# Softmax attentions with the maximum as ScalarE's bias and four output strips; a state-space step with its D term on TensorE

## Chip, cores, metric

One Trainium2 core runs the kernel. The metric is device time in microseconds (us) of the whole program; lower is better.

## What is computed

X holds 32 batches of 128 tokens with 128 numbers each. Six stages follow one another, and each ends with a layer norm over the last axis; cut to what the change touches:

```python
x = _layernorm(x + _L0_attn_ref(x, wq, wk, wv, wo))   # 1: 16 heads of 8, RoPE, causal
x = _layernorm(x + _L0_xattn_ref(ctx_1024, x, ...))   # 2: linear attention block
x = _layernorm(x + _L0_ffn_ref(x, ...))               # 3: routed experts
x = _layernorm(x + _L1_attn_ref(x, ...))              # 4: state space, below
x = _layernorm(x + _L1_xattn_ref(x, ctx_1024, ...))   # 5: 16 heads, 77 context keys
x = _layernorm(x + _L1_ffn_ref(x, ...))               # 6: experts chosen by sinkhorn

# 1 and 5, per batch and head
attn = softmax(Q @ K.T * scale + mask);  out = (attn @ V) @ wo.T

# 4: h is 256 x 16 numbers a batch, a recurrence over the 128 tokens
h = h * dA + dt_t * B_t * u_t;  y = einsum('bdn,bn->bd', h, C_t)
y = y_all + xc * D_param;  y = y * silu(z)
return x + y @ W_out                  # the caller adds x once more: 2 x + y @ W_out
```

All values are float32.

## The kernel before

X stays in SBUF. Every stage works on NG = 8 groups of GB = 4 batches, and each of the engines has a program of its own; semaphores link them. The first group of a stage is written out in a prelude, the others come from a loop body that also starts the next group.

**The attentions** (stage 1, names a_, and stage 5, names k_, one function `attention`) go through a group in 8 units u: half of the 16 heads of one batch. The order on each engine is written out by hand. TensorE forms the scores of 8 heads in two PSUM banks (L512; L515 adds the causal mask in stage 1), two units ahead. VectorE (`less_max`) takes the maximum of each head (L378, or L372 and L374 with the context's mask), then subtracts it and writes DD (L380, L376). ScalarE turns DD into E by one Exp over all 8 heads (L278). TensorE transposes E (L522), ScalarE copies the result to PT (L311), and TensorE multiplies by V (`outputs`, L533, 8 matmuls a unit into two strips of 32 columns of its array). VectorE sums E (L384). ScalarE does copy u, then Exp u + 1; the transposition of u + 1 waits for that Exp. One projection of the next group shares a unit's slot on TensorE (L490, L499 in stage 1, in units 1 to 5), its rotation by RoPE follows on VectorE (L391), and POOL builds the block-diagonal keys BD and the masked queries QM. In stage 5 ScalarE writes QM (L300). At a group's end come the reciprocal of the sums, the scaling of the outputs (rT on ScalarE, oT on VectorE L440), the matmuls by wo (L586), Y, statistics (L72), POOL's power and the norm (L90).

In the trace most float32 matmuls show up as two records (L533 as x16 for 8), transpositions as one.

**The state space** (stage 4, names m_, `state_space`) runs 32 steps per group, two channels (CH) by 16 states, through `pipeline`. Everything else of a group is hung on the steps by the table SLOT, which gives each part of the work a step number. A step: TensorE spreads B and C over the partitions (L1532, L1539), VectorE multiplies in PSUM by DU (L1447) and scans (L1452), ScalarE makes dA (L1405), POOL multiplies h by C (L1317), TensorE adds that up in a PSUM bank per channel (L1559, by the identity). After the last step of a group VectorE adds the D term (`gated`, L1457), multiplies by silu(z) (`gate`, L1462), TensorE projects (`output`), VectorE adds 2 X (`residual`, L1466), takes statistics (L72), POOL raises to the power, and VectorE normalises (`norm`, L90). These stand among the first steps of the next group.

**Openings.** In stage 1 a first block issues all of its loads on SP's queue and sets constants, then the prelude starts; POOL sets V to zero (L241) ahead of copying X. The four projections go through one bank, so each waits for the rotation before it. In stage 4 POOL folds the norm's weight into the convolution (L1290) ahead of the first inner norm, and `early` for group 1 runs ahead of step 0.

## Time and profile before

| what | value |
| --- | --- |
| median of 3 runs | 2200.84 us (2200.73 to 2204.45) |
| profiled execution | 2199.49 us, span 2197.7 us |
| mean granted TensorE clock | 0.867 |
| busy: TensorE, VectorE, ScalarE, POOL | 1684.6, 1584.7, 957.9, 826.3 us |
| stage 1, 2, 3 | 0 to 341, 341 to 600, 600 to 782 us |
| stage 4, 5, 6 | 782 to 1497, 1497 to 1784, 1784 to 2197.7 us |

The busy times are sums over stages that have different limits, so the table gives the frame only. A stage's limit is read from its own window: the busy time of each engine against the window's length, then who waits for whom inside one unit or one step. PEclk is the mean clock that TensorE was granted, 1.00 for 2.4 GHz and 0.50 for 1.2 GHz.

### The profile page before, as it was taken

What the parts mean: (1) busy time and instruction counts of PE and PEld (TensorE: products, weight loads), DVE (VectorE), ACT (ScalarE), POOL (GpSimd) and SP (SyncE); (2) the same over time, 40 slices, a digit from 0 to 9 for tenths busy, and PEclk for the clock granted to TensorE, in tenths of its full rate; (3) what the DMA queues carried; (4) which work ended last, traced back from release to release, by engine and by line L of the source; (5) the groups of instructions that cost most, each with busy time, mean ns of one, the idle gap of its engine ahead of it and who ended that gap; (6) DMA issues with size and microseconds to landing.
All of it is one profiled execution on the core that took longest, in us unless ns stands there. A gap on an engine that the chain in (4) does not pass through costs nothing. (4 is left out here: it accounts for less than half of the span.)

```text
span 2197.7 us, 31301 instructions
## 1 busy us (share of the span) xinstructions
PE 1684.6 (77%) x10064; PEld 1101.4 (50%) x10064; DVE 1584.7 (72%) x3014; ACT 957.9 (44%) x1509; POOL 826.3 (38%) x855
## 2 busy tenths in 40 slices
PE   6999986888699947777778778766999871289992
PEld 3555556877466622223223223214666661188882
DVE  3999995566478827988888888894989947833335
ACT  1444452454545435564564664643555432011114
POOL 2222211333300025665665665663222100066653
PEclk9999997788799968788888888897999975599996
DMA  4000000000000000000000000000000040076664
GB/s 127 1 0 0 0 1 24 1 1 2 1 1 0 0 10 0 1 0 2 0 0 1 0 0 0 0 0 10 7 3 6 1 130 0 9 232 204 198 203 122
DMA packets 48580, 71.47 MB, mean 33 GB/s; under 512 B 8877, under 2 KB 34581, under 8 KB 48197
## 3 DMA queue, kind: packets, MB, share of 16 engines
q1 hardware_dynamic: 43909, 60.64, 8.7%
q0 software_dynamic: 4544, 9.32, 1.5%
q8 instruction: 58, 0.95, 0.2%
q14 instruction: 69, 0.57, 0.1%
HBM read 58.46 MB, written 11.47 MB: 32 GB/s over the span
## 5 line engine op out<-in xcount | busy, mean ns | idle before, releaser
L1559 PE MATMUL PS<-m_hC,identf 128*128 128x512 f32 x512 | 330.0, 731 | 147.4 <-POOL m_hC L1317 142.2
L1317 POOL TENSOR_TENSOR m_hC<-m_h,m_Cs 128x512 f32<-128x512 f32 x256 | 337.1, 1325 | 223.9 <-DVE m_h L1452 154.3
L1452 DVE TENSOR_TENSOR_SCAN m_h<-m_dA,PS 128x512 f32<-128x512 f32 x256 | 312.4, 1220 | 29.6 <-ACT m_dA L1405 18.7
L1559 PEld LDWEIGHTS PS<-m_hC,identf 128*128 128x128 f32 x512 | 102.1, 223 | 289.9 <-POOL m_hC L1317 264.2
L1447 DVE TENSOR_TENSOR PS<-PS,m_DU 128x512 f32<-128x512 f32 x256 | 178.3, 697 | 29.5 <-PE PS L1532 16.3
L1405 ACT ACTIVATE m_dA<-m_DT,m_A 128x508 f32<-128x508 f32 x256 | 177.9, 716 | 28.5 <-DVE m_h L1452 22.5
L1410 ACT COPY m_Cs<-PS 128x512 f32<-128x512 f32 x128 | 74.2, 580 | 264.9 <-PE PS L1539 264.9
L1992 PE MATMUL PS<-e_xT,e_WT 128*128 128x128 f32 x1136 | 145.1, 282 | 13.0 <-DVE e_xT L1892 11.9
L1992 PEld LDWEIGHTS PS<-e_xT,e_WT 128*128 128x128 f32 x1136 | 136.4, 196 | 18.6 <-DVE e_xT L1892 17.3
L1765 ACT ACTIVATE e_Sg<-PS 128x512 f32<-128x512 f32 x71 | 42.3, 597 | 225.6 <-PE PS L1992 158.7
L1701 POOL DMA_INDIRECT e_XG<-token_rows,e_ids x71 | 68.8, 969 | 159.3 <-DVE e_ids L1886 138.0
L82 POOL TENSOR_TENSOR ln_lv<-ln_mv,ln_eps 128x4 f32<-128x4 f32 x32 | 6.4, 200 | 319.3 <-DVE ln_mv L75 319.3
L311 ACT COPY a_PT<-PS 128x1024 f32<-128x1024 f32 x63 | 63.8, 1012 | 88.1 <-PE PS L522 88.1
L1899 DVE TENSOR_TENSOR e_HT<-PS,e_Sg 128x512 f32<-128x512 f32 x71 | 49.1, 691 | 69.5 <-PE PS L1992 56.9
L1706 POOL DMA_INDIRECT expert_rows<-e_Yo,e_ids x71 | 69.9, 985 | 74.6 <-DVE e_Yo L1905 64.1
L278 ACT ACTIVATE a_E<-a_DD 128x1024 f32<-128x1024 f32 x64 | 67.7, 1057 | 55.0 <-DVE a_DD L380 53.8
L311 ACT COPY k_PT<-PS 77x1024 f32<-77x1024 f32 x63 | 63.4, 1007 | 61.8 <-PE PS L522 61.8
L522 PE MATMUL PS<-identf,k_E 128*77 128x128 f32 x512 | 71.4, 283 | 15.0 <-ACT k_E L278 14.9
L378 DVE TENSOR_REDUCE a_mx<-PS 128x8 f32<-128x1024 f32 x64 | 77.3, 1207 | 7.7 <-PE PS L515 7.7
L384 DVE TENSOR_REDUCE a_sm<-a_E 128x8 f32<-128x1024 f32 x64 | 77.4, 1210 | 5.4 <-ACT a_E L278 5.4
L1209 PEld LDWEIGHTS PS<-w_ew,f_G 128*128 128x128 f32 x512 | 64.7, 191 | 32.2 <-issue 26.0
L380 DVE TENSOR_TENSOR a_DD<-PS,a_mx 128x1024 f32<-128x1024 f32 x64 | 78.4, 1224 | 2.2
(374 smaller groups left out, 3926.4 us busy)
## 6 DMA issues: line engine op xcount, KB each, us to landing
e_WT<-in_w_wgu SPq DMA_DIRECT2D x71, 512.0 KB
token_rows<-X SPq DMA_DIRECT2D x2, 2048.0 KB
e_Y<-expert_rows SPq DMA_DIRECT2D x16, 256.0 KB, 3.9
e_w_wd<-in_w_wd SPq DMA_DIRECT2D x1, 2048.0 KB, 8.3
out_dram<-X SPq DMA_DIRECT2D x8, 256.0 KB, 2.3
X<-in_x SPq DMA_DIRECT2D x1, 1792.0 KB, 7.6
x_Cs<-in_ctx SPq DMA_DIRECT2D x8, 154.0 KB
k_Cs<-in_ctx SPq DMA_DIRECT2D x8, 154.0 KB
```

What stands on the lines that cost most here:

```text
L311: nc.scalar.copy(PT[:, u % 2], PS[0:KL, 4:6, :].rearrange("p i (h q) -> p (i h) q", q=P)).then_inc(s["pt"], 1)
L378: nc.vector.tensor_reduce(m, units(hf), AX_X, ALU.max).then_inc(s["mx"], 1)
L380: nc.vector.tensor_tensor(d, units(hf), mb, ALU.subtract).then_inc(s["d"], 1)
L384: nc.vector.tensor_reduce(sm[:, u * HU:(u + 1) * HU], E[:, u % 2], AX_X, ALU.add).then_inc(s["sm"], 1)
L522: ins = nc.tensor.transpose(PS[0:KL, 4 + h // 4, (h % 4) * P:(h % 4 + 1) * P], E[:, u % 2, h, :], c.identf[:, :])
L1317: nc.gpsimd.tensor_tensor(hC[:, i % ND, :], hst[:, i % ND, :], Cs[:, n % ND, :], ALU.mult).then_inc(s["hC"], 1)
L1405: nc.scalar.activation(dA[:, i % ND, :, 1:P], bl(DT[:, par, ch, :])[:, :, 1:P], ACT.Exp, scale=A[:, ch, n:n + 1]).then_inc(s["dA"], 1)
L1410: nc.scalar.copy(Cs[:, n % ND, :], bank(3)).then_inc(s["Cs"], 1)
L1447: nc.vector.tensor_tensor(bank(4), bank(1 + n % 2), DU[:, par, ch, :], ALU.mult).then_inc(s["dBu"], 1)
L1452: nc.vector.tensor_tensor_scan(hst[:, i % ND, :], dA[:, i % ND].rearrange("p b l -> p (b l)"), bank(4), 0.0, ALU.mult, ALU.add).then_inc(s ...
L1559: nc.tensor.matmul(bank(5 + ch), c.identf[:, :], hC[:, i % ND, :], start=(n == 0), stop=(n == NS - 1)).then_inc(s["yacc"], 1)
L1992: ins = nc.tensor.matmul(PS[:, banks[i % 2], f * P:(f + 1) * P], WT[:, i % RW, w, f * P:(f + 1) * P], xT[:, i % 2, :], start=True, stop=True)
```

## The change

Softmax. For the upper 4 of a unit's 8 heads VectorE only takes the maximum and multiplies it by -SCALE (a new 128x4 operation, nmx); ScalarE takes this as the bias of four Exps, one for each head, that read the scores themselves (PSUM in stage 1, DD with the mask in stage 5). For the lower 4 heads subtraction and Exp stay, at half size. `outputs` runs once per batch, after its second unit, as 16 matmuls over four strips in turn; PT has four buffers. The maxima of both first units of the next group stand ahead of oT on VectorE.

Stage 4. The D term is a matmul by a diagonal matrix Dp that opens each channel's accumulation, and 2 X comes from a matmul by `twice` that opens the projection's. VectorE keeps the product by silu(z), from PSUM, and statistics from PSUM. ScalarE does the norm of the group, with POOL making its bias by two small products more. The channels of the convolution's projection change places.

Openings. V is set to zero by VectorE; the first projections have banks of their own and don't wait for a rotation; in stage 1 loads are split over SP's and ScalarE's queues, and the separate first block is gone; in stage 4 the fold comes after the first inner norm, and `early` for group 1 after step 0 (VectorE), 1 (POOL), 3 (TensorE) or 4 (ScalarE). ScalarE loads its Exp table early. `keep_warm` issues 9 to 14 bf16 matmuls of 128x512 into an unused bank at the start of stages 1 and 4 and at the end of stages 1, 2, 4 and 5.

```diff
+def keep_warm(c, n, at):
+    for i in range(n):
+        nc = c.nc
+        nc.tensor.matmul(c.PS[:, at, :], c.warm[:, 0:P], c.warm[:, :], start=True, stop=True)
...
-    for stages, g in ((early, 0), (prepare, 0), (early, 1)):
+    for stages in (early, prepare):
         for stage in stages.values():
-            stage(g, g)
-    for i in range(shift):
-        step(0, 0, i, 2)
+            stage(0, 0)
+    for i in range(-1, shift):
+        if i >= 0:
+            step(0, 0, i, 2)
+        if i == second:
+            for stage in early.values():
+                stage(1, 1)
...
-    PT = sb("PT", [KL, 2, HU, P])
+    PT = sb("PT", [KL, 4, HU, P])
...
-                nc.gpsimd.memset(V[:, :, :, :], 0.0).then_inc(s["z"], 1)
...
             def exps(g, u):
+                act.wait_ge(s["nm"], g * UN + u + 1)
+                for j in range(HG):
+                    src = DD[:, u % 2, HG + j, :] if cross else PS[:, 2 * (u % 2) + 1, j * KL:(j + 1) * KL]
+                    nc.scalar.activation(E[:, u % 2, HG + j, :], src, ACT.Exp, bias=nmx[:, u % 2, j:j + 1], scale=SCALE)
                 act.wait_ge(s["d"], g * UN + u + 1)
-                nc.scalar.activation(E[:, u % 2], DD[:, u % 2], ACT.Exp, scale=SCALE).then_inc(s["e"], 1)
+                nc.scalar.activation(E[:, u % 2, 0:HG], DD[:, u % 2, 0:HG], ACT.Exp, scale=SCALE).then_inc(s["e"], 1)
...
+                act.wait_ge(s["o_ready"], g * GB + u // 2)
+                nc.scalar.copy(PT[:, u % 4], PS[0:KL, 4:6, :].rearrange("p i (h q) -> p (i h) q", q=P)).then_inc(s["pt"], 1)
...
-                    dve.wait_ge(s["mx"], at)
-                    nc.vector.tensor_tensor(d, d, mb, ALU.subtract).then_inc(s["d"], 1)
                 else:
                     nc.vector.tensor_reduce(m, units(hf), AX_X, ALU.max).then_inc(s["mx"], 1)
-                    dve.wait_ge(s["mx"], at)
-                    nc.vector.tensor_tensor(d, units(hf), mb, ALU.subtract).then_inc(s["d"], 1)
+                dve.wait_ge(s["mx"], at)
+                nc.vector.tensor_scalar(nmx[:, hf, :], mx[:, hf, HG:HU], -SCALE, 0.0, ALU.mult, ALU.add).then_inc(s["nm"], 1)
+                nc.vector.tensor_tensor(DD[:, hf, 0:HG], DD[:, hf, 0:HG] if cross else scores(2 * hf), mb, ALU.subtract).then_inc(s["d"], 1)
...
+                nc.vector.memset(V[:, :, :, :], 0.0).then_inc(s["zv"], 1)
+                dve.wait_ge(s["zv"], 1)
                 dve.wait_ge(wsem, wcount)
-                dve.wait_ge(s["z"], 2)
+                if cross:
+                    values(0, 0, FIRST_V + 1)
+                else:
+                    for i in range(4):
+                        rotate(0, i, i)
+                    dve.wait_ge(s["rot"], 4)
+                    nc.vector.tensor_tensor(QM[:, 0, :], R[:, 2, :], R[:, 3, :], ALU.add).then_inc(s["q"], 1)
                 if xsem is not None:
                     dve.wait_ge(xsem[0], 16)
...
                         if left:
                             less_max(g + 1, 1 - par, 0)
+                            less_max(g + 1, 1 - par, 1)
                     if left:
                         if cross:
...
                 if left:
-                    less_max(g + 1, 1 - par, 1)
...
-            def outputs(g, par, u):
-                hf, b = u % 2, u // 2
-                pe.wait_ge(s["pt"], g * UN + u + 1)
-                if u == 0:
+            def outputs(g, par, b):
+                pe.wait_ge(s["pt"], g * UN + 2 * b + 2)
+                if b == 0:
                     pe.wait_ge(s["v"], g + 1)
-                for h in [i % 2 * HG + i // 2 for i in range(HU)]:
-                    gp, j = 2 * hf + h // HG, h % HG
-                    ins = nc.tensor.matmul(PS[32 * gp:32 * gp + 32, OUT, b * P:(b + 1) * P], V[:, par, b * 4 + gp, 32 * j:32 * j + 32], PT[:, u % 2, h, :],
-                                           start=(j == 0), stop=(j == HG - 1))
+                for j in range(HG):
+                    for gp in range(4):
+                        ins = nc.tensor.matmul(PS[32 * gp:32 * gp + 32, OUT, b * P:(b + 1) * P], V[:, par, b * 4 + gp, 32 * j:32 * j + 32],
...
+                else:
+                    pe.wait_ge(s["xT"], 1)
+                    for i, w in enumerate(("wk", "wkp", "wq", "wqp")):
+                        nc.tensor.matmul(bank(i), W[w][:, :], xT[:, :], start=True, stop=True).then_inc(s["kp"], 1)
+                    project_values(0, FIRST_V)
...
                         ins.then_inc(s["rTp"], 1)
-                    outputs(g, par, u)
+                    if u % 2 == 0:
+                        outputs(g, par, u // 2 - 1)
                 if left:
                     pe.wait_ge(s["pt"], g * UN + UN)
                     transpose_p(g + 1, 0)
+                outputs(g, par, GB - 1)
+                if left:
...
+            keep_warm(c, 14, 0)
...
-    SLOT = {"gated": 1, "silu_z": 1, "gate": 2, "output0": 2, "output1": 3, "rstd": 5, "residual": 6, "norm": 7,
+    SLOT = {"silu_z": 1, "gate": 1, "output0": 2, "output1": 3, "rstd": 5, "stats": 5, "norm": 9,
...
+                if isinstance(g, int) and g == 0:
+                    fold()
...
+                for ch in range(CH):
+                    nc.scalar.activation(Dp[:, ch, :], c.identf[:, :], ACT.Copy, scale=W["dp"][:, ch:ch + 1]).then_inc(s["tw"], 1)
+                nc.scalar.activation(twice[:, :], c.identf[:, :], ACT.Copy, scale=2.0).then_inc(s["tw"], 1)
...
+            def norm(g, par):
+                act.wait_ge(s["nb"], g + 1)
+                for b in range(GB):
+                    ins = nc.scalar.activation(X[:, bass.ds(g * GB + b, 1), :].rearrange("p o d -> p (o d)"), PS[:, 7, b * D:(b + 1) * D], ACT.Identity, scale=ln["rs"][:, b:b + 1], bias=no[:, 1, b:b + 1])
+                ins.then_inc(s["x"], 1)
...
-            def gated(g, par):
+            def gate(g, par):
                 dve.wait_ge(s["yacc"], g * NI + NI)
+                dve.wait_ge(s["sz"], g + 1)
                 for ch in range(CH):
-                    nc.vector.scalar_tensor_tensor(YG[:, ch, :], U2[:, par, ch, :], W["dp"][:, ch:ch + 1], bank(5 + ch), ALU.mult, ALU.add).then_inc(s["y1"], 1)
-            def gate(g, par):
-                dve.wait_ge(s["y1"], g * 2 + 2)
-                dve.wait_ge(s["sz"], g + 1)
-                nc.vector.tensor_tensor(YG[:, :, :], YG[:, :, :], SZ[:, par], ALU.mult).then_inc(s["y2"], 1)
-            def residual(g, par):
+                    nc.vector.tensor_tensor(YG[:, ch, :], bank(5 + ch), SZ[:, par, ch, :], ALU.mult).then_inc(s["y1"], 1)
+            def out_stats(g, par):
                 dve.wait_ge(s["yp"], g + 1)
-                nc.vector.scalar_tensor_tensor(flat(Xn[:, :, :]), flat(group(c, g)), 2.0, bank(7), ALU.mult, ALU.add).then_inc(s["r2"], 1)
-                dve.wait_ge(s["r2"], g + 1)
-                ln_stats(dve, nc, Xn, ln, s, g + 1)
-            def norm(g, par):
-                ln_apply(dve, nc, group(c, g), Xn, ln, s, g + 1, s["x"])
+                ln_stats(dve, nc, bl(bank(7)), ln, s, g + 1)
...
                         pe.wait_ge(s["xnT"], g + 1)
-                        if not isinstance(g, int) or g > 0:
-                            pe.wait_ge(s["zc"], g * CH)
+                    if ch == 0 and half == 0 and (not isinstance(g, int) or g > 0):
+                        pe.wait_ge(s["zc"], g * CH)
+                        pe.wait_ge(s["x"], g)
...
-                if n == 0 and not (isinstance(g, int) and g == 0):
-                    pe.wait_ge(s["y1"], g * 2 - 1 + ch)
+                if n == 0:
+                    if not (isinstance(g, int) and g == 0):
+                        pe.wait_ge(s["y1"], g * 2 - 1 + ch)
+                    nc.tensor.matmul(bank(5 + ch), Dp[:, ch, :], U2[:, par, ch, :], start=True, stop=False)
                 pe.wait_ge(s["hC"], g * NI + i + 1)
-                nc.tensor.matmul(bank(5 + ch), c.identf[:, :], hC[:, i % ND, :], start=(n == 0), stop=(n == NS - 1)).then_inc(s["yacc"], 1)
+                nc.tensor.matmul(bank(5 + ch), c.identf[:, :], hC[:, i % ND, :], start=False, stop=(n == NS - 1)).then_inc(s["yacc"], 1)
...
+                    pe.wait_ge(s["y1"], g * 2 + 2)
                     for b in (2 * half, 2 * half + 1):
+                        nc.tensor.matmul(PS[:, 7, b * D:(b + 1) * D], twice[:, :], X[:, bass.ds(g * GB + b, 1), :].rearrange("p o d -> p (o d)"), start=True, stop=False)
                         for ch in range(CH):
-                            ins = nc.tensor.matmul(PS[:, 7, b * D:(b + 1) * D], YG[:, ch, b * P:(b + 1) * P], W["wout"][:, ch, :], start=(ch == 0), stop=(ch == CH - 1))
+                            ins = nc.tensor.matmul(PS[:, 7, b * D:(b + 1) * D], YG[:, ch, b * P:(b + 1) * P], W["wout"][:, ch, :], start=False, stop=(ch == CH - 1))
...
+            keep_warm(c, 12, 1)
...
-        def later_loads(sp):
+        def first_load(eng, *names):
+            for n in names:
+                eng.dma_start(Ws[1][n][:, :], dram[f"w1_{n}"]).then_inc(sem[1], 16)
+        def first_sp(sp):
+            sp.dma_start(c.X[:, 0:GB, :], dram["x"][:, 0:GB, :]).then_inc(s_x, 16)
+            first_load(sp, "wk", "wq", "cos", "hmask", "wv", "wo")
...
+        def first_act(act):
+            nc.scalar.dma_start(c.identf[:, :], dram["identf"]).then_inc(s_identity, 16)
+            first_load(nc.scalar, "wkp", "wqp", "sin", "cmask")
...
+        def first_pe(pe):
+            pe.wait_ge(s_warm, 1)
+            keep_warm(c, 9, 6)
+            pe.wait_ge(s_identity, 16)
```

Order of instructions on TensorE within a group of stage 1, units 2 and 3, before (a_E are the exponentials, a_PT their transposed copy, PS is PSUM):

```order
L533 MATMUL PS<-a_PT,a_V 32x128 x8
L520 REGISTER_ALU
L522 MATMUL PS<-identf,a_E 128x128 x8
L512 MATMUL PS<-a_BD,a_QM 128x512 x2
L515 MATMUL PS<-w_cmask,identb 128x512 x2
L489 REGISTER_ALU
L490 MATMUL PS<-a_xT,w_wq 128x512
L533 MATMUL PS<-a_PT,a_V 32x128 x8
L520 REGISTER_ALU
L522 MATMUL PS<-identf,a_E 128x128 x8
L512 MATMUL PS<-a_BD,a_QM 128x512 x2
```

and in the changed kernel:

```order
L557 MATMUL PS<-a_PT,a_V 32x128 x16
L545 REGISTER_ALU
L547 MATMUL PS<-identf,a_E 128x128 x8
L537 MATMUL PS<-a_BD,a_QM 128x512 x2
L540 MATMUL PS<-w_cmask,identb 128x512 x2
L513 REGISTER_ALU
L514 MATMUL PS<-a_xT,w_wq 128x512
L545 REGISTER_ALU
L547 MATMUL PS<-identf,a_E 128x128 x8
L537 MATMUL PS<-a_BD,a_QM 128x512 x2
L540 MATMUL PS<-w_cmask,identb 128x512 x2
L513 REGISTER_ALU
```

One call of the output matmuls now has 16 of them, and the unit that follows has none.

ScalarE in the same stage, two units, before:

```order
L311 COPY a_PT<-PS 128x1024
L277 REGISTER_ALU
L278 ACTIVATE a_E<-a_DD 128x1024
L311 COPY a_PT<-PS 128x1024
L277 REGISTER_ALU
L278 ACTIVATE a_E<-a_DD 128x1024
```

and in the changed kernel:

```order
L327 COPY a_PT<-PS 128x1024
L329 REGISTER_ALU
L289 REGISTER_ALU
L292 ACTIVATE a_E<-PS,a_nmx 128x128 x4
L294 ACTIVATE a_E<-a_DD 128x512
L326 REGISTER_ALU
L327 COPY a_PT<-PS 128x1024
L289 REGISTER_ALU
L292 ACTIVATE a_E<-PS,a_nmx 128x128 x4
L294 ACTIVATE a_E<-a_DD 128x512
```

Between two copies there stood one Exp, and now there are five in two forms, the four small ones behind VectorE's a_nmx.

VectorE behind the last step of a group in stage 4, before:

```order
L1451 REGISTER_ALU
L1452 SCALAR_TENSOR_TENSOR m_h<-m_dA,PS 128x512
L1457 SCALAR_TENSOR_TENSOR m_YG<-m_U,w_dp,PS 128x512 x2
L1444 REGISTER_ALU
L1447 TENSOR_TENSOR PS<-PS,m_DU 128x512
L1448 REGISTER_ALU
L1451 REGISTER_ALU
L1452 SCALAR_TENSOR_TENSOR m_h<-m_dA,PS 128x512
L1462 TENSOR_TENSOR m_YG<-m_YG,m_SZ 128x1024
```

and some steps later, the residual, the statistics and the first of four norms:

```order
L1466 ISA
L1466 SCALAR_TENSOR_TENSOR m_Xn<-X,PS 128x512
L72 BN_STATS ln_st<-m_Xn 128x6 x4
L75 BN_AGGR ln_mv<-ln_st 128x2 x4
L1447 TENSOR_TENSOR PS<-PS,m_DU 128x512
L1448 REGISTER_ALU
L1452 SCALAR_TENSOR_TENSOR m_h<-m_dA,PS 128x512
L90 TENSOR_SCALAR X<-m_Xn,ln_mv,ln_rs 128x128
L90 ISA
```

In the changed kernel the same two places on VectorE read:

```order
L1512 REGISTER_ALU
L1513 SCALAR_TENSOR_TENSOR m_h<-m_dA,PS 128x512
L1519 TENSOR_TENSOR m_YG<-PS,m_SZ 128x512 x2
L1505 REGISTER_ALU
L1508 TENSOR_TENSOR PS<-PS,m_DU 128x512
L1509 REGISTER_ALU
L1512 REGISTER_ALU
L1513 SCALAR_TENSOR_TENSOR m_h<-m_dA,PS 128x512
```

and, for the second, the statistics straight from PSUM:

```order
L1508 TENSOR_TENSOR PS<-PS,m_DU 128x512
L1509 REGISTER_ALU
L1513 SCALAR_TENSOR_TENSOR m_h<-m_dA,PS 128x512
L72 BN_STATS ln_st<-PS 128x6 x4
L75 BN_AGGR ln_mv<-ln_st 128x2 x4
L1505 REGISTER_ALU
L1508 TENSOR_TENSOR PS<-PS,m_DU 128x512
L1509 REGISTER_ALU
```

The product by m_SZ moved up from the second step to the first and absorbed the D term's place; m_Xn, the residual and the norm's L90 are gone from this engine.

## Rows read from the trace of the kernel before

**Rows 1.** Busy time by engine; window, length, busy and count each, clock, DMA.

```profile
79.60:335.10 255.50, 236.99 (x1842) 142.02 (x1842) 232.76 (x294) 121.91 (x129) 58.08 (x62) 0.99 0.00 0
793.30:803.50 10.20, 10.13 (x16) 4.04 (x16) 0.00 (x0) 1.97 (x2) 0.00 (x0) 0.70 0.00 0
926.00:1490.80 564.80, 422.21 (x952) 163.82 (x950) 488.12 (x603) 299.90 (x464) 344.76 (x270) 0.84 0.00 0
1554.30:1778.70 224.40, 200.52 (x1736) 151.78 (x1736) 201.37 (x348) 119.74 (x159) 53.87 (x63) 0.99 0.01 4
```

**Rows 2.** Timeline, stage 1: start, length, engine, work, [idle before].

```profile
135.54 1.07 PE L533 MATMUL PS<-a_PT,a_V 128*32 128x128 f32 x16
...
136.54 1.09 PE L522 MATMUL PS<-identf,a_E 128*128 128x128 f32 x8
...
141.05 1.09 PE L522 MATMUL PS<-identf,a_E 128*128 128x128 f32 x8
...
142.18 1.01 ACT L311 COPY a_PT<-PS 128x1024 f32<-128x1024 f32 x1 [2.30 <-PE PS L522]
...
143.08 1.06 ACT L278 ACTIVATE a_E<-a_DD 128x1024 f32<-128x1024 f32 x1
```

**Rows 3.** ScalarE by form: busy us, mean ns, idle before, releasers.

```profile
L278 ACT ACTIVATE a_E<-a_DD 128x1024 f32<-128x1024 f32 x64 | 67.7, 1057 | 55.0 <-DVE a_DD L380 53.8
...
L278 ACT ACTIVATE k_E<-k_DD 128x616 f32<-128x616 f32 x64 | 45.9, 718 | 48.2 <-DVE k_DD L376 47.3
...
L1773 ACT ACTIVATE e_Y<-e_Y,e_E 128x128 f32<-128x128 f32 x32 | 10.1, 387 | 10.8 <-DMA e_Y<-expert_rows 10.8
```

**Rows 4.** VectorE by form, the same columns.

```profile
L380 DVE TENSOR_TENSOR a_DD<-PS,a_mx 128x1024 f32<-128x1024 f32 x64 | 78.4, 1224 | 2.2
...
L376 DVE TENSOR_TENSOR k_DD<-k_DD,k_mx 128x616 f32<-128x616 f32 x64 | 55.4, 866 | 2.2
...
L90 DVE TENSOR_SCALAR X<-m_Xn,ln_mv,ln_rs 128x128 f32 x24 | 16.0, 726 | 0.0
...
L90 DVE TENSOR_SCALAR X<-a_Y,ln_mv,ln_rs 128x128 f32 x24 | 6.7, 342 | 0.0
```

**Rows 5.** Timeline, stage 5, two plain units and the queries.

```profile
1599.40 2.77 ACT L300 ACTIVATE k_QM<-PS,k_bqm,w_gmask 128x512 f32<-128x512 f32 x4
...
1604.25 1.10 PE L522 MATMUL PS<-identf,k_E 128*77 128x128 f32 x8
...
1607.44 1.10 PE L522 MATMUL PS<-identf,k_E 128*77 128x128 f32 x8
```

**Rows 6.** Timeline of VectorE, end of one group of stage 4.

```profile
1083.20 1.41 DVE L1457 SCALAR_TENSOR_TENSOR m_YG<-m_U,w_dp,PS 128x512 f32<-128x512 f32 x2 [1.01 <-PE PS L1559]
...
1086.47 1.20 DVE L1462 TENSOR_TENSOR m_YG<-m_YG,m_SZ 128x1024 f32<-128x1024 f32 x1
...
1095.55 0.66 DVE L1466 SCALAR_TENSOR_TENSOR m_Xn<-X,PS 128x512 f32<-128x512 f32 x1
...
1099.34 2.67 DVE L90 TENSOR_SCALAR X<-m_Xn,ln_mv,ln_rs 128x128 f32 x4
```

**Rows 7.** Costliest groups of the page, the one that sums in PSUM.

```profile
L1559 PE MATMUL PS<-m_hC,identf 128*128 128x512 f32 x512 | 330.0, 731 | 147.4 <-POOL m_hC L1317 142.2
```

**Rows 8.** Timeline, opening of stage 1.

```profile
7.29 4.36 POOL L241 MEMSET a_V<- 128x5120 f32 x1
...
29.00 2.08 PE L512 MATMUL PS<-a_BD,a_QM 32*128 32x512 f32 x4
```

**Rows 9.** Timeline, opening of stage 4.

```profile
785.36 2.34 POOL L1290 TENSOR_TENSOR m_Wc<-m_Wc,w_win 128x1024 f32<-128x1024 f32 x1 [3.52 <-DMA m_Wc<-in_w_cwr]
...
830.51 0.70 DVE L1447 TENSOR_TENSOR PS<-PS,m_DU 128x512 f32<-128x512 f32 x1 [6.37 <-PE PS L1532]
```

**Rows 10.** Timeline, opening of stage 5.

```profile
1496.77 4.36 POOL L241 MEMSET k_V<- 77x5120 f32 x1
...
1513.80 1.75 PE L512 MATMUL PS<-k_BD,k_QM 128*128 128x308 f32 x3
```

181 lines of the change are left out of this document (97 added, 84 removed).

## Prediction

> **What bounds the kernel now.** I read the windows first (busy time per engine in the steady part of three stages), then the timeline of single units inside them, then the rows of the operations that the change touches, and last the three openings. Everything is summed against the profiled execution, 2199.49 us (span 2197.7); the median of the runs is 2200.84, so 1.35 us is added at the end. A measurement of this kernel tells about 0.2% (4.4 us) from no change.
>
> In stage 1 [rows 1] seven groups take 255.50 us (36.5 each). TensorE is busy 236.99 of it and VectorE 232.76: two engines at over 90%, ScalarE under half. So neither limit alone can be removed with profit. Stage 5 is the same picture at 224.40 us (32.1 a group), 200.52 and 201.37. In stage 4 seven groups take 564.80 us (80.7 each); VectorE is busy 488.12, TensorE 422.21, POOL 344.76, ScalarE 299.90. VectorE leads, and its idle 76.7 us (11 a group) are waits on others. TensorE's accumulation there waits 147.4 us, 142.2 of them for POOL's product [rows 7], and POOL's product waits for VectorE's scan: time given back by VectorE goes down this line.
>
> In stage 1 the units come in two kinds. Where a projection shares the slot, TensorE runs without a gap, 4.51 us from one transposition to the next, of which the output matmuls take 1.00 [rows 2]. Where there is none, VectorE's three passes of about 1.22 [rows 4] make 3.66. Beside both runs a loop of ScalarE and TensorE: transposition at 141.05, copy 142.18, Exp 143.08, which needs 1.06, then the next transposition: 2.03 + 1.06 + 0.07 of release = 3.16, hidden so far. In stage 5 the plain units stand 3.19 apart [rows 5].
>
> **Attentions, ScalarE's part.** Two Exps of different sizes [rows 3] give the slope: (1057 - 718) / (1024 - 616) = 0.83 ns an element, 0.21 us fixed. The half left over costs 0.63 (512 elements) or 0.46 (308). A 128x128 piece with one pointer operand has a row, 387 ns, so 0.28 fixed; of 77 elements, 0.345. Neighbours overlap by about 0.1: four queries of 771 ns would be 3.08 and take 2.77 [rows 5], with [rows 3] giving the fixed part. So stage 1: 4x0.387 + 0.63 - 0.4 = 1.78, +0.72 over 1.06. Stage 5: 4x0.345 + 0.46 - 0.4 = 1.44, +0.72 over 0.72. Without overlap each is 0.4 more (bound above). The loop becomes 2.03 + 1.78 + 0.07 = 3.88 in stage 1 and 3.54 in stage 5.
>
> **VectorE's part.** The subtraction halves: 1.22 to about 0.66, 0.87 to about 0.46. Added is the 128x4 scaling of the maximum. It has no row: below it costs nothing, above the 0.34 us of L90's 32 times larger scaling. I take 0.1, nearer the first, plus a chance to wait for POOL. The rows for that are L90's too: the same operation on the same shape takes 342 ns behind the attention and 726 in stage 4 [rows 4]; POOL is busy 23% and 61% of those windows [rows 1]. At 23% I take 0.1 us more a unit. Net -0.35 a unit in stage 1, -0.2 in stage 5. A plain unit of stage 1 then costs VectorE 3.66 - 0.35 = 3.31, less than the loop's 3.88: it no longer bounds.
>
> The Trainium skill, page "SBUF — State Buffer", says that VectorE and GpSimd arbitrate for one port pair by an exclusive lock held for the full instruction. The two L90 rows agree. Read strictly it speaks against this change: each of 128 new scalings could stand behind one whole GpSimd instruction, and ScalarE waits for it.
>
> **TensorE's part.** Two units have 32 records of output matmuls, before in two calls over two strips each, now in one over four strips. Two strips give 16 records in 1.00 [rows 2]. Four are bounded by no better rate (2.0 for 32) and by twice the rate (1.0); I take 1.3 against 2.0, nearer the second. So two units with projections: before 9.02. After, the one without outputs is no longer PE's 3.51 but the loop's 3.88; the other is 3.51 + 1.3 = 4.81. Together 8.69, -0.33; two such pairs, -0.66. Plain units: 3.66 to 3.88, +0.22, three of them, +0.66. At the boundary both maxima of the next group now stand ahead of oT, so the VectorE wait for ScalarE's rT is filled: the order shows it, and I take -0.6. Per group -0.6, over seven **-4**.
>
> The Trainium skill, page "TensorEngine Tiling (Array Packing)", section Theoretical Speedup, gives 4x tiling for a small dimension of 32 and "Up to 4×". By it 32 matmuls would take the 1.0 of my lower bound, and the stage would gain 0.3 more per pair. No row here shows four strips, so the trace can't confirm it.
>
> Stage 5: plain units 3.19 to 3.54, three a group, +1.05. The queries (2.77 on ScalarE) lie between one Exp and the next copy; they were just covered, and an Exp that ends 0.72 later pushes the copy by that: +0.7. Output slots -0.35, boundary -0.2. +1.2 a group, **+9** over seven (rounded up for the last).
>
> **Stage 4.** Gone from VectorE per group [rows 6]: the D term 1.41, the gate 1.20, the residual 0.66, the last norm 2.67, 5.94 in all. New: two half gates, by the size of the old one 2x0.7 = 1.4. Net -4.5 busy. The statistics read PSUM in place of SBUF at the same price. The norm's slot is also one in which POOL and VectorE collided (726 against 342), so some more comes back from POOL; I take -5.2 a group, **-36** over seven. What arrives elsewhere: TensorE gets two 128x512 matmuls, four records at 0.64 (330.0 over 512, [rows 7]), and four small ones, about 3.5 us of the 20 us a group that it is idle; ScalarE gets four norms, some 0.4 each as the piece with one pointer, 1.6 of 38 idle. If either stands ahead of a step, it takes part back: ends -20 and -42.
>
> **Openings.** Stage 1: the memset of V holds POOL 4.36 us from 7.29, and the copy of X that starts everything stands behind it; the four projections then wait for each rotation; the first score comes at 29.00 [rows 8]. With the load order, four banks and the sum of the queries on VectorE I follow: X at about 4 (an estimate: half of what stands ahead of it now), transposed and copied by 6.5, four projections until 15 if each takes the 2.08 that the score takes at the low clock, rotation and sum to 16: -13. The first scores, 2.08 each now, may run at the full clock, and the first group has the new slots: -4. VectorE's memset of 5120 elements must end before its first rotation; at 1.2 ns an element it would take 6 us from 1, just hidden. **-17** (-12 to -22).
>
> Stage 4: the fold of the convolution (POOL waits 3.52 and works 2.34, [rows 9]) leaves the chain to the inner norm; its statistics are ready within the first part: -4.2. Sixteen projections run 10.13 us at a mean clock of 0.70 [rows 1]; at full clock 7.1: -3. VectorE's first step waits 6.37 for TensorE, which stands behind the second group's transposition; now that comes after some steps: -5 of 6.37. **-12** (-9 to -14).
>
> Stage 5: the same memset 4.36 ahead of X [rows 10]; the score at 1513.80. Memset -4.3; of the 12.7 us that then remain until the score, an earlier table load and separate banks take about a third, -4.5 (an estimate, no row has them apart); less 2 for the first group's longer Exps: **-7** (-5 to -10).
>
> Filler matmuls at the ends of stages 1, 2, 4 and 5: 9 to 14 short ones in a time in which TensorE had nothing. They can give only what the low clock cost later; by the 3 us of stage 4 I take **-4** in all for stages 2, 3 and 6, ends 0 and -10.
>
> **Sum.** -4 + 9 - 36 - 17 - 12 - 7 - 4 = -71. 2199.5 - 71 = 2128.5, plus 1.35 is about 2130; I say 2129.
>
> **Rivals.**
> 1. As summed, 2129: chance 0.52. Its own range is 2112 to 2146.
> 2. VectorE's relief in stage 4 is half eaten. For it: TensorE waits 142.2 us for POOL [rows 7], VectorE already idles 11 us a group. A POOL backlog, or the D matmul ahead of a step's sum, would take the VectorE time as a wait. Against it: POOL is only 61% busy. The stage gives -20 in place of -36: 2145. Chance 0.18.
> 3. The attentions go below the sum: four strips cost the lower bound, and VectorE's relief counts in full. 0.35 us a unit over 64 units is 22 less in stage 1, and the +9 vanishes: 2100. Against it is the loop of 3.88. Chance 0.11.
> 4. The attentions get slower by the loop: the pieces do not overlap, +0.4 in each unit that the loop bounds, about half of 128: +26, 2155. For it: nothing in the trace has Exps with a pointer on PSUM back to back. Against it: the queries' 2.77 for four. Chance 0.14.
> 5. Slower than before: the loop's place is ScalarE between copy and transposition, 128 times. To eat the -71 it must cost 0.55 us a unit more than summed (71/128), that is Exp parts of 2.3 us in stage 1 with every other term right. With each scaling stuck behind a whole POOL product, which holds ScalarE back by the same time, that could be 0.65 a unit: 2129 + 83 = 2212. The rows speak against it, as POOL is busy 23% there. Chance 0.04.
> 6. The change does little: stage 4 limited by POOL, openings by the loads. 2200. Chance 0.01.
>
> **Numbers.** The range takes in cases 1 to 4 but for their outer ends: 2095 to 2162. Faster by over 0.2%: 0.95; within: 0.01; slower: 0.04.
>
> **What would show it.** Right: the plain units of stages 1 and 5 stand 3.9 and 3.5 apart with ScalarE, not VectorE, released last; 32 output matmuls in 1.3; a stage 4 group at about 75.5; first score near 16. Wrong: scaling rows of over 0.3 us, output matmuls at 2 us for 32, stage 4 still over 78 a group with more idle time before VectorE's sum or TensorE's accumulation, or stage 1 at 34 a group, where I have put the loop too high. The biggest single term is stage 4's; an error there of half its size is more than all openings' bounds together.

## The result and the profile after

The changed kernel takes 2143.74 us (median of 4 runs, 2141.09 to 2149.92) against 2202.62 for the kernel before in the same comparison: ratio 0.9737, 95% interval 0.9712 to 0.9761. That is 58.9 us less, where 71 were forecast; it lies inside the range. The profiled execution was the longest of the four, 2149.92 us with a span of 2148.1, while that of the kernel before (2199.49) was shorter than any of the four beside it (2200.73 to 2204.45). So the two traces differ by 49.6 us, and the other 9.3 are in no stretch below.

The trace of both kernels was cut at the same instructions: the first and the last sum Y of an attention, the first inner statistics, the first step and the first and last gate of stage 4, the first Exp of stage 5, the first copy of an expert's rows.

| stretch | before | after | moved | forecast |
| --- | --- | --- | --- | --- |
| start to first Y of stage 1 | 79.6 | 59.9 | -19.7 | -17 |
| seven groups of stage 1 | 255.5 | 250.7 | -4.8 | -4 |
| from there to stage 4 | 446.9 | 445.8 | -1.1 | part of -4 |
| opening of stage 4 to the first step | 48.5 | 35.7 | -12.8 | -12 |
| first step to first gate | 82.4 | 84.8 | +2.4 | none |
| seven groups of stage 4 | 573.1 | 550.4 | -22.7 | -36 |
| last gate to first Y of stage 5 | 68.3 | 63.5 | -4.8 | -7 |
| seven groups of stage 5 | 224.4 | 239.0 | +14.6 | +9 |
| from there to stage 6's expert rows | 148.3 | 145.1 | -3.2 | part of -4 |
| stage 6's experts to the end | 270.7 | 273.2 | +2.5 | none |

The three steady stretches in the changed kernel's trace (window, length, busy time and count of TensorE, its weight loads, VectorE, ScalarE and POOL, then clock and DMA). Stages 1 and 5 before are in [rows 1]. The window of stage 4 in [rows 1] runs from the first to the last statistics of the output (564.80 us); cut at the gates as the table has it, the kernel before gives the first line here:

```profile
912.90:1486.00 573.10, 429.52 (x969) 166.78 (x968) 498.67 (x615) 305.14 (x472) 351.10 (x275) 0.85 0.00 1
```

```profile
59.90:310.60 250.70, 220.37 (x1858) 125.67 (x1860) 211.88 (x347) 152.19 (x344) 58.14 (x62) 0.96 0.00 1
876.90:1427.30 550.40, 432.87 (x1053) 168.47 (x1052) 469.29 (x574) 314.37 (x500) 349.08 (x289) 0.88 0.00 0
1490.80:1729.80 239.00, 179.25 (x1752) 132.85 (x1754) 192.01 (x400) 157.16 (x374) 51.18 (x63) 0.97 0.01 4
```

In stage 1 VectorE lost 20.9 us of work and TensorE 16.6, and the time only 4.8. In stage 5 TensorE lost 21.3 and VectorE 9.4, and the stage grew, while ScalarE went from 119.74 to 157.16. The operations behind it, ScalarE by form (busy us, mean ns, idle before):

```profile
L292 ACT ACTIVATE a_E<-PS,a_nmx 128x128 f32<-128x128 f32 x256 | 73.4, 374 | 20.8 <-DVE a_nmx L397 20.0
L292 ACT ACTIVATE k_E<-k_DD,k_nmx 128x77 f32<-128x77 f32 x256 | 71.0, 352 | 18.6 <-DVE k_nmx L397 17.9
...
L294 ACT ACTIVATE a_E<-a_DD 128x512 f32<-128x512 f32 x64 | 41.7, 651 | 0.0
...
L294 ACT ACTIVATE k_E<-k_DD 128x308 f32<-128x308 f32 x64 | 28.6, 448 | 0.0
```

and VectorE's new and halved ones:

```profile
L398 DVE TENSOR_TENSOR a_DD<-PS,a_mx 128x512 f32<-128x512 f32 x64 | 43.7, 682 | 0.0
L398 DVE TENSOR_TENSOR k_DD<-k_DD,k_mx 128x308 f32<-128x308 f32 x64 | 30.6, 478 | 0.0
...
L397 DVE TENSOR_SCALAR k_nmx<-k_mx 128x4 f32<-128x4 f32 x64 | 17.1, 268 | 2.2
...
L397 DVE TENSOR_SCALAR a_nmx<-a_mx 128x4 f32<-128x4 f32 x64 | 14.0, 219 | 2.2
```

The forecast had 387 and 345 ns for a piece of 128 and 77 elements, 0.63 and 0.46 us for the rest, and for the scaling 0.1 bare with 0.1 more for POOL. The pieces are right (374 and 352 ns, 0.65 and 0.45 us), the scaling takes 0.22 and 0.27 us. Two plain units of stage 5 (units without a projection), from the timeline:

```profile
1542.70 1.10 PE L547 MATMUL PS<-identf,k_E 128*77 128x128 f32 x8
...
1543.84 1.01 ACT L327 COPY k_PT<-PS 77x1024 f32<-77x1024 f32 x1 [1.19 <-PE PS L547]
1544.74 1.11 ACT L292 ACTIVATE k_E<-k_DD,k_nmx 128x77 f32<-128x77 f32 x4
...
1545.75 0.45 ACT L294 ACTIVATE k_E<-k_DD 128x308 f32<-128x308 f32 x1
...
1546.25 1.10 PE L547 MATMUL PS<-identf,k_E 128*77 128x128 f32 x8 [1.41 <-ACT k_E L294]
1546.54 0.17 DVE L397 TENSOR_SCALAR k_nmx<-k_mx 128x4 f32<-128x4 f32 x1
...
1548.32 1.08 PE L557 MATMUL PS<-k_PT,k_V 77*32 77x128 f32 x32
...
1549.88 1.10 PE L547 MATMUL PS<-identf,k_E 128*77 128x128 f32 x8 [0.48 <-ACT k_E L294]
```

From one transposition to the next it is 3.55 and 3.63 us: copy, four Exps on the bias, one Exp, transposition. ScalarE is released by TensorE and TensorE by ScalarE, while VectorE's scaling for the next unit (at 1546.54) is done 1.7 us before it is wanted. Before, two such units stood 3.19 apart [rows 5]. This holds for plain units: over each attention ScalarE's first Exp still waited 15 times for the scaling, 20.0 and 17.9 us in all (the rows of L292 above). The line with x32 answers to the x16 of [rows 2]: 32 records of output matmuls in 1.08 us where 16 took 1.07.

VectorE at the end of a stage 4 group, which answers to [rows 6]:

```profile
1040.97 1.29 DVE L1519 TENSOR_TENSOR m_YG<-PS,m_SZ 128x512 f32<-128x512 f32 x2 [0.93 <-PE PS L1616]
...
1050.68 0.89 DVE L72 BATCH_NORM_STATS2 ln_st<-PS 128x6 f32<-128x128 f32 x4 [0.44 <-PE PS L1624]
```

Four pieces of work with 5.94 us became one with 1.29. The first score of stage 1 stands at 15.91, against 29.00 in [rows 8]:

```profile
4.43 0.61 POOL L235 COPY a_Xs<-X 128x512 f32<-128x512 f32 x1 [3.60 <-DMA X<-in_x]
...
7.10 1.10 PE L574 MATMUL PS<-a_xT,w_wk 128*128 128x512 f32 x2 [0.77 <-ACT a_xT L298]
...
9.75 1.02 PE L574 MATMUL PS<-a_xT,w_wqp 128*128 128x512 f32 x2
...
15.91 1.36 PE L537 MATMUL PS<-a_BD,a_QM 32*128 32x512 f32 x4 [4.24 <-POOL a_BD L247]
```

X is copied at 4.43, the projections follow one another without a rotation in between and at the full clock, and what holds the score is POOL's BD, not the projections. In stage 4 the first step no longer waits for TensorE [rows 9] but for POOL's product:

```profile
792.13 0.70 DVE L1508 TENSOR_TENSOR PS<-PS,m_DU 128x512 f32<-128x512 f32 x1 [2.46 <-POOL m_DU L1354]
```

### The profile page after: what moved, and what is told of

Its sections match the earlier page's. It is cut to its first block and busy times, and to the rows that moved or that the text cites. A ratio compares the mean times of both kernels' runs of the same rounds, so it can differ in the third digit from the quotient of the medians.

```text
span 2148.1 us, 32305 instructions
## 1 busy us (share of the span) xinstructions
PE 1651.6 (77%) x10228; PEld 1063.9 (50%) x10233; DVE 1525.8 (71%) x3098; ACT 1049.6 (49%) x2056; POOL 813.2 (38%) x868
## 5 line engine op out<-in xcount | busy, mean ns | idle before, releaser
L1362 POOL TENSOR_TENSOR m_hC<-m_h,m_Cs 128x512 f32<-128x512 f32 x256 | 332.6, 1307 | 216.4 <-DVE m_h L1513 152.0
L1616 PE MATMUL PS<-m_hC,identf 128*128 128x512 f32 x512 | 319.9, 710 | 116.3 <-POOL m_hC L1362 115.7
L547 PEld LDWEIGHTS PS<-identf,k_E 128*77 128x77 f32 x512 | 56.5, 149 | 75.4 <-ACT k_E L294 53.9
L327 ACT COPY k_PT<-PS 77x1024 f32<-77x1024 f32 x63 | 63.5, 1008 | 56.9 <-PE PS L547 56.9
L547 PE MATMUL PS<-identf,a_E 128*128 128x128 f32 x512 | 72.7, 287 | 23.3 <-ACT a_E L294 21.7
L292 ACT ACTIVATE a_E<-PS,a_nmx 128x128 f32<-128x128 f32 x256 | 73.4, 374 | 20.8 <-DVE a_nmx L397 20.0
```

What stands on the lines that cost most here:

```text
L292: nc.scalar.activation(E[:, u % 2, HG + j, :], src, ACT.Exp, bias=nmx[:, u % 2, j:j + 1], scale=SCALE)
L327: nc.scalar.copy(PT[:, u % 4], PS[0:KL, 4:6, :].rearrange("p i (h q) -> p (i h) q", q=P)).then_inc(s["pt"], 1)
L547: ins = nc.tensor.transpose(PS[0:KL, 4 + h // 4, (h % 4) * P:(h % 4 + 1) * P], E[:, u % 2, h, :], c.identf[:, :])
L1362: nc.gpsimd.tensor_tensor(hC[:, i % ND, :], hst[:, i % ND, :], Cs[:, n % ND, :], ALU.mult).then_inc(s["hC"], 1)
L1616: nc.tensor.matmul(bank(5 + ch), c.identf[:, :], hC[:, i % ND, :], start=False, stop=(n == NS - 1)).then_inc(s["yacc"], 1)
```

## The experiments

The runs came in three sets of four, and the kernel before ran on the same chip as each set: 2173.41 us (median) beside the first, 2173.47 beside the second and 2199.75 beside the third. So ratios are compared between sets, and microseconds only inside a set or inside a stretch of a trace. A stretch is read from one execution each: the one from stage 1 to stage 4, which no experiment but the one without fillers edits, took 441.0 to 445.9 us in the twelve traces, so a difference of a few microseconds in one stretch needs more than one trace to stand. The sets are: the changed kernel again, the old end, the bias in stage 1 alone, the filler; then no bias, both gains, tail and order, no filler matmuls; then the rest.

**The changed kernel again.** No edit.

> The changed kernel once more, nothing edited, as the yardstick of its neighbours and for a second profile. Its first profiled execution took 2149.92 us and its median was 2143.74. Theory: the 6 us between them lie in stage 4, where the groups alternate between 79.3 us at a clock of 0.89 and 84.8 at 0.84, so an execution with other dips is shorter there by a multiple of about 5.5. Rival: they lie in stage 6, where the profile was 2.5 us longer than that of before. Median expected at 2144.

Median 2120.07 us where 2144 was expected, ratio 0.975 (0.9728 to 0.9773). Every stretch but one repeats within 3.5 us: stage 1 250.5, stage 4 549.2, stage 5 240.7. The last one, stage 6's experts, took 243.6 in place of 273.2; these 29.6 us are the whole difference between the two traces (spans 2148.1 and 2118.7), and no edit touches that stage. The 6 us between the first profile and its median are not placed by this, neither by the theory nor by its rival: stage 4 gave only 1.2.

**The old end of a stage 4 group.**

```diff
-    SLOT = {"silu_z": 1, "gate": 1, "output0": 2, "output1": 3, "rstd": 5, "stats": 5, "norm": 9,
+    SLOT = {"gated": 1, "silu_z": 1, "gate": 2, "output0": 2, "output1": 3, "rstd": 5, "residual": 6, "norm": 7,
...
-                    nc.tensor.matmul(bank(5 + ch), Dp[:, ch, :], U2[:, par, ch, :], start=True, stop=False)
...
-                        nc.tensor.matmul(PS[:, 7, b * D:(b + 1) * D], twice[:, :], X[:, bass.ds(g * GB + b, 1), :]...)
```

with `gated`, `gate`, `residual` and `norm` on VectorE as before, and the norm gone from ScalarE.

> The changed kernel with the end of a stage 4 group as it was: D term, gate, residual and norm on VectorE, no matmuls by Dp and twice. If the change of this part is worth what the two profiles say (573.1 against 550.4 us over seven groups), it is 20 to 25 us slower than the changed kernel, about 2167. If the gain of the whole came from the openings and the part was worth the -36 that was forecast, only hidden by something else, 2180. If VectorE's relief is worth nothing there, 2145. Its groups should take 82 to 85 us again with 71 to 72 us of VectorE busy in each.

Median 2148.96, 28.9 above its neighbour; ratio 0.9884 (0.9864 to 0.9904). The seven groups take 580.7 us against 549.2: by these two traces the part is worth **31.5 us**, by the medians 28.9, near the 36 of the forecast. The profiled execution (2156.62) was the longest of its four. And 580.7 is 7.6 above the 573.1 of the kernel before, which has the same tail. One group of it:

```profile
882.20:967.50 85.30, 65.60 (x145) 25.81 (x144) 72.47 (x91) 46.27 (x72) 52.00 (x42) 0.82 0.00 1
```

**Tail and order of the channels.** The same with the projections of channel 0 first:

```diff
-                      "x0": project_x(1, 0), "x1": project_x(1, 1), "x2": project_x(0, 0), "x3": project_x(0, 1)
+                      "x0": project_x(0, 0), "x1": project_x(0, 1), "x2": project_x(1, 0), "x3": project_x(1, 1)
```

> The old end of a stage 4 group on the changed kernel took 580.7 us over seven groups, 7.6 more than the kernel before, which has the same tail. Here the projections of the convolution go back to channel 0 first as well. If the order of channels costs the 7.6, the seven groups take 573; if it is the clock that falls otherwise, they stay between 578 and 583, and the clock of the groups says so.

Median 2149.13, ratio 0.9889 (0.9866 to 0.9911), seven groups 580.6: the order costs nothing. In the kernel before, two of the first five groups took 82.3 us at a clock of 0.85 and three 85.0 to 85.2 at 0.82, with the same 72.5 us of VectorE; with the old tail under the new opening all five take 85.1 to 85.5. The changed kernel has such pairs too:

```profile
956.20:1041.00 84.80, 67.21 (x157) 26.23 (x156) 68.41 (x86) 47.58 (x76) 51.72 (x44) 0.84 0.00 0
1041.00:1120.20 79.20, 62.23 (x157) 24.64 (x156) 68.28 (x86) 47.71 (x76) 51.74 (x44) 0.89 0.00 0
```

84.8 and 79.2 us for the same work on VectorE. So in the one trace of the kernel before two groups had a better clock. Both profiles with the old tail were the longest of their four executions, and that of the kernel before was a short one; how many such groups the other executions have isn't known. So the part is worth 29 to 32 us by its reversal and 22.7 by the two first profiles, and the 7.6 between them are a difference between single executions.

**A filler in stage 4.**

```diff
                 if not first(g, n, 1):
                     pe.wait_ge(s["Cs"], g * NS + n)
+                keep_warm(c, 1, 3)
```

> The changed kernel with one bf16 matmul of 128x512 more ahead of each spreading of C in stage 4, into the bank that it is about to overwrite: 16 a group, some 0.21 us each at the full clock. Theory, the clock: groups at 0.89 take 79.3 us and those at 0.84 take 84.8 with the same VectorE work, so if the fillers keep the clock up, up to 5 us in every second group is won, 5 to 25 us in all, and the mean clock of the stage rises from 0.88 towards 1.0. Rival, TensorE's time: 16 matmuls add 3.4 us a group to TensorE, 27 in all, and the time grows by 5 to 25.

Median 2110.83, 9.2 below its neighbour; ratio 0.9712 (0.9695 to 0.9728). Two groups:

```profile
876.10:955.10 79.00, 63.05 (x172) 25.81 (x172) 68.18 (x86) 46.97 (x76) 51.64 (x43) 0.94 0.00 1
955.10:1037.80 82.70, 67.14 (x172) 27.32 (x172) 68.12 (x86) 47.38 (x76) 51.66 (x43) 0.86 0.00 1
```

The seven groups take 544.9 us, 4.3 less, at a mean clock of 0.92 against 0.88. The other 5 us of the medians aren't in the edited stage. The theory holds in its sign; its size, 5 to 25 us, is just missed. TensorE's busy time is 430.6 us against 430.2, with 110 records more. And the mean clock of a group doesn't tell its time: the fourth group took 82.0 us at 0.94, and the first 79.0 at the same 0.94.

```profile
1116.10:1198.10 82.00, 63.02 (x173) 25.58 (x172) 68.25 (x87) 47.64 (x76) 51.67 (x43) 0.94 0.00 0
```

**The bias in stage 1 alone.** In stage 5:

```diff
+                if cross:
+                    act.wait_ge(s["d"], g * UN + u + 1)
+                    nc.scalar.activation(E[:, u % 2], DD[:, u % 2], ACT.Exp, scale=SCALE).then_inc(s["e"], 1)
+                    return
```

and the subtraction over all eight heads on VectorE.

> The changed kernel, but in stage 5 VectorE subtracts the maximum for all eight heads and ScalarE takes one Exp of 616 elements, as before the change; stage 1 keeps its bias. Theory: the loop of ScalarE and TensorE bounds stage 5 (3.55 and 3.63 us a unit in the profile against 3.19 before), so it is faster by 10 to 22 us: the four strips stay and the longer Exps go. A group then takes 31 to 32 us in place of 34.0. Rival, VectorE bounds it: its 0.27 us scaling goes and 0.4 comes back, so the time stays within 3 us or grows.

Median 2096.77, 23.3 below its neighbour; ratio 0.9642 (0.9622 to 0.9661). Stage 5's seven groups fall from 240.7 to 223.4 us, 17.3 less. Of this the last group alone gives 6.3 (35.2 to 28.9). One group with the bias (the changed kernel), then one without:

```profile
1524.80:1558.70 33.90, 26.24 (x256) 19.26 (x256) 28.13 (x59) 23.54 (x56) 8.11 (x10) 1.00 0.02 5
```

```profile
1517.70:1549.60 31.90, 26.10 (x256) 19.26 (x256) 29.61 (x51) 17.73 (x24) 8.61 (x10) 1.00 0.02 5
```

VectorE works 1.5 us more and ScalarE 5.8 less, and the group is 2.0 shorter. So it is ScalarE's part, not VectorE's sum. Everything else that the change did to stage 5 is worth 224.4 - 223.4 = 1.0, and more where the clock holds: two of the seven groups here were at 0.95, and in the run with both gains (below), where none was, they took 221.1.

**No bias at all.** The same for both attentions.

> The changed kernel with the whole subtraction on VectorE and one Exp for eight heads in both attentions; strips, order and openings stay. Stage 5 is known from its neighbour: 223.4 us for seven groups against 240.7. Open is stage 1. If the bias pays there, its seven groups go from 250.5 back to 255 or more. If, as in stage 5, the loop of ScalarE costs more than VectorE gets back, and the 4.8 us won in stage 1 came from the four strips, they go below 250.5, to about 242. As a ratio to the kernel before: 0.966 in the first case, 0.960 in the second.

Median 2106.35, ratio 0.9696 (0.9675 to 0.9718). Stage 1 takes 259.2 us against 250.5, so here the bias is worth 8.7. That sum has three parts: 1.4 us in each of the first six groups at the full clock (8.4), some 3 for two groups more at a lower clock in this run, and 2.7 the other way, as the last group took 33.4 without the bias and 36.1 with it. The first two groups behind the opening without it, and the same two with it:

```profile
62.20:100.40 38.20, 33.32 (x272) 19.18 (x272) 34.48 (x43) 17.99 (x19) 9.40 (x10) 0.96 0.01 2
100.40:137.00 36.60, 31.91 (x272) 17.88 (x272) 34.50 (x44) 17.99 (x19) 9.40 (x10) 1.00 0.00 0
```

```profile
62.20:97.40 35.20, 31.79 (x272) 17.90 (x272) 31.34 (x52) 22.50 (x51) 9.41 (x10) 1.00 0.00 1
97.40:134.30 36.90, 33.59 (x272) 19.13 (x272) 31.40 (x52) 22.41 (x51) 9.40 (x10) 0.95 0.00 0
```

At the full clock it is 36.6 against 35.2, and before the change 37.2. Each kind has groups with a dip, a short stretch at 1.2 GHz, that takes the mean clock to 0.95 or 0.96, in which 1.6 to 1.7 us more pass, with VectorE's work unchanged. The kernel before had a clock of 1.00 in its first six groups.

**The scaling twice.**

```diff
+                nc.vector.tensor_scalar(nmx2[:, hf, :], mx[:, hf, HG:HU], -SCALE, 0.0, ALU.mult, ALU.add)
                 nc.vector.tensor_scalar(nmx[:, hf, :], mx[:, hf, HG:HU], -SCALE, 0.0, ALU.mult, ALU.add).then_inc(s["nm"], 1)
```

> The changed kernel with VectorE's scaling of the maximum issued twice, the first time into a buffer that nobody reads: 0.17 to 0.27 us more of VectorE in each of 128 units, ahead of ScalarE's bias. If VectorE, or the wait of ScalarE for the scaling, bounds the units, stages 1 and 5 grow by 0.2 a unit, 13 us each. If the loop of ScalarE and TensorE bounds them, the scaling of the next unit is done long before the copy of this one, and each grows by less than 4. In stage 5 plain units the scaling ends 1 us ahead of the Exp that needs it, so I expect the second there; in stage 1 VectorE is nearer, some 5 us.

Median 2155.31, ratio 0.9805 (0.9788 to 0.9822). A steady group of stage 1 and one of stage 5:

```profile
62.20:97.60 35.40, 31.78 (x272) 17.88 (x272) 31.81 (x60) 22.54 (x51) 9.42 (x10) 1.00 0.01 1
1596.50:1631.30 34.80, 26.22 (x256) 19.26 (x256) 29.66 (x68) 23.54 (x56) 7.71 (x10) 1.00 0.02 5
```

35.4 against 35.2, and 34.8 against 33.9. The doubled scaling costs 0.2 us in a stage 1 group and 0.9 in one of stage 5, where 8 times 0.17 to 0.27 would be 1.4 to 2.1. So VectorE is not the bound of stage 1's units, where I had expected some 5 us in all and none came (250.3 against 250.5). In stage 5 about half of it comes through, more than the 4 us that I had set as the bound (seven groups 246.6 in place of 240.7). So VectorE isn't free there: the waits of ScalarE's first Exp for the scaling went from 15 times and 17.9 us in the changed kernel to 21 times and 21.8 us. The ratio grew by about 12 us; the profile places 6 to 8 of them.

**No filler matmuls.** `keep_warm` issues none.

> The changed kernel with none of the filler matmuls (starts of stages 1 and 4, ends of stages 1, 2, 4 and 5). Forecast: 4 us slower, between 0 and 10. Where each acts is read from the openings: 35.7 in stage 4 (3 of them by the clock), 145 from the last group of stage 5 to the first rows of stage 6, 60 to the first output of stage 1. The rival is that the clock rises at the same moment anyway, then it is within 1 us.

Median 2125.48, ratio 0.9791 (0.9765 to 0.9817). The ratio is 0.004 or 9 us above the changed kernel's, with intervals that overlap; the medians lie 5.4 apart, with the kernel before at the same median beside both, and the two traces 4.0. So the fillers' worth as a whole is on the edge of noise. By stretch: opening of stage 4 38.2 against 35.8, stage 5's 38.9 against 37.3, into stage 6 148.5 against 147.0, first Y 63.7 against 62.2. In the opening of stage 1 the cause is in the rows: the first projection (at 6.68) took 2.05 us, where it took 1.10 with the fillers. Against these 7 us, stage 1's groups took 247.5 in place of 250.5, with none of the first six at a lower clock. So where the dips of the clock fall is not fixed by the work of a group.

**The second group's early parts first.**

```diff
+    second = -1
     for i in range(-1, shift):
```

> The changed kernel with the early parts of the second group ahead of step 0 again on all engines, as before the change. Opening of stage 4 (first statistics to first step) 35.8 us now; forecast of this term was -5, so it should be 40.8 here, and the first group, 83.9, should lose its extra work, to 82. Sum +3. The rival: the first step waits for POOL's product anyway and nothing moves.

Median 2146.62, ratio 0.9768 (0.9748 to 0.9787). The opening takes 40.9 and the first group 81.4: 5.1 lost, 2.5 won back, as expected. The 5.1 are clear, as ten of the other traces with the changed opening have 35.7 or 35.8 in this stretch, one 36.2 and the one without fillers 38.2; the first group varies from 82.8 to 84.8 in runs that don't touch it, so of the 2.5 some may be chance. In the whole the edit is not told apart from the changed kernel (0.975). VectorE's first step again has the wait of [rows 9]:

```profile
796.74 0.70 DVE L1509 TENSOR_TENSOR PS<-PS,m_DU 128x512 f32<-128x512 f32 x1 [6.38 <-PE PS L1588]
```

**Both gains together.** The bias in stage 1 alone and the filler in stage 4. The next two experiments start from this kernel.

> The changed kernel with both edits that gave time: stage 5 without the bias (-23 alone) and a filler matmul ahead of each spreading of C in stage 4 (-9 alone). They touch different stages, so by either theory they add: ratio to the kernel before 0.9642 - 0.0038 = 0.960. If the whole depends on a common clock budget, less than the sum, 0.963.

Median 2094.09, ratio 0.9632 (0.9603 to 0.9662): the lowest ratio of all, below the kernel before and the changed kernel, with intervals that don't touch. From the bias edit alone (0.9642) it is not told apart, and its interval holds both forecasts (0.960 and 0.963). In the trace both gains are there, stage 4 at 544.9 us and stage 5 at 221.1.

**Fillers in the last group.** On the kernel with both gains:

```diff
+                    if not left and u < UN - 1:
+                        if u == 1:
+                            pe.wait_ge(s["yr"], g)
+                        keep_warm(c, 3, AUX)
```

> The kernel of e_s5_fill with three filler matmuls a unit (128x512, bf16) in the last group of both attentions, where there is no projection for TensorE. The last group of stage 1 took 35.8 to 36.2 us in all kernels with the bias and 31.9 before the change, at a clock of 0.80 with 0.50 in places. If the clock is what it loses, it falls to 32 or 33 and the whole by 3 to 4 us. If it is the loop of ScalarE and TensorE (8 times 3.9 is 31, and the group's end comes on top), it stays at 35 to 37, and the fillers may add to it.

Median 2120.06, ratio 0.9646 (0.9628 to 0.9663), not told apart from the kernel with both gains. The last group of stage 1 takes 35.1 us in place of 35.8, at a clock of 0.90 in place of 0.80; that of stage 5, without a bias in both, 29.8 in place of 28.9. So the clock alone isn't what the last group lost. Three things make up its 4.2 us (31.9 before, 36.1 in the changed kernel; they come to 4.6, with 0.4 won elsewhere). These transpositions of the last group show the first two, before and after:

```profile
308.87 1.06 PE L522 MATMUL PS<-identf,a_E 128*128 128x128 f32 x8 [1.80 <-ACT a_E L278]
...
313.41 1.07 PE L522 MATMUL PS<-identf,a_E 128*128 128x128 f32 x8 [0.88 <-ACT a_E L278]
```

```profile
279.77 1.94 PE L547 MATMUL PS<-identf,a_E 128*128 128x128 f32 x8 [2.84 <-ACT a_E L294]
...
286.44 1.09 PE L547 MATMUL PS<-identf,a_E 128*128 128x128 f32 x8
...
294.11 1.07 PE L547 MATMUL PS<-identf,a_E 128*128 128x128 f32 x8
...
297.93 1.06 PE L547 MATMUL PS<-identf,a_E 128*128 128x128 f32 x8 [1.16 <-ACT a_E L294]
```

One unit at the low clock took 6.67 us (279.77 to 286.44) where it took 4.54. The later ones, with no projection beside them, stand 3.82 apart, where they stood 3.24 to 3.62: that is the loop, about 1.2 in all. And from the last transposition to Y it is 8.85 against 7.58, at the low clock for longer. With the fillers this end is 6.61, but the units are longer: 7.06, 4.25, 4.25, 3.85 and 3.82.

**Two fillers a step in stage 4.** On the kernel with both gains, `keep_warm(c, 2, 3)` in place of one.

> The kernel of e_s5_fill with two fillers ahead of each spreading of C in stage 4 in place of one. One filler took the seven groups from 549 to 545 at a clock of 0.89 to 0.92. If more activity still buys clock, 540; if TensorE's own time now counts, 548 to 560, since 16 more of 0.21 are 3.4 us a group.

Median 2126.54, ratio 0.9659 (0.964 to 0.9679); the seven groups take 551.2 us. The second filler gives back what the first had won. The clock is not what it lost, as its mean rose from 0.92 to 0.95; TensorE's busy time rose from 433.2 to 445.3 us, so it is most likely TensorE's own time.

## Why the prediction was right, point by point

It was right in time and sign; 71 was forecast, 59 came. Part of this is luck: stage 4 brought less and stage 5 cost more than forecast, the openings brought a little more, and stage 1 came out right by errors against each other. The signs of being right were 3.9 and 3.5 us between plain units (3.82 and 3.55 came), 1.3 for 32 output records (1.08), a stage 4 group at 75.5 (78.6), and the first score near 16 (15.91). The 75.5 was counted from 80.7, the seventh part of 564.80 in [rows 1], a window that ends with the last statistics; from gate to gate a group took 81.9, so 76.7 is the forecast in the table's marks. "Over 78" was a sign of being wrong only with more idle time, and TensorE's ahead of its accumulation fell from 147.4 to 116.3 us.

**ScalarE's loop.** Right as a mechanism. 2.03 + 1.44 + 0.07 = 3.54 was forecast for a plain unit of stage 5 and 3.55 measured; overlap of neighbours 0.1, pieces as worked out. In stage 1 it was 3.88 and 3.82.

**Stage 5.** +9 was forecast and +14.6 came. A group inside the stage went from 32.4 to 33.9, +1.5 where +1.2 was forecast: two plain units +0.8, the two units beside the queries +0.5, the rest +0.2. The step that failed is "(rounded up for the last)". The last group, where no projection hides the loop, went from 29.4 to 34.8, +5.4 alone. The bias is what it lost: without it the same group takes 28.9, and all seven 223.4 in place of 240.7.

**Four strips.** Mis-sized: I took 1.3 and 1.08 was measured, near the lower bound. By the Trainium skill, page "TensorEngine Tiling (Array Packing)", section Theoretical Speedup, a dimension of 32 gives up to 4x. The part of it that this trace can show agrees: from two strips to four the rate doubled, 16 records in 1.07 and 32 in 1.08. Stage 5 did not get the difference, since the loop bounds its plain units and TensorE idles there.

**The scaling and the port.** I took 0.1 bare and 0.1 more for POOL. Measured are 0.17 bare and 0.05 and 0.10 more in the mean, 0.22 and 0.27. Three of them in the timeline of VectorE, two with the work of POOL beside them:

```profile
1528.20 0.61 POOL L235 COPY k_Xs<-X 128x512 f32 x1
1528.40 0.43 DVE L397 TENSOR_SCALAR k_nmx<-k_mx 128x4 f32<-128x4 f32 x1
...
1532.51 0.17 DVE L397 TENSOR_SCALAR k_nmx<-k_mx 128x4 f32<-128x4 f32 x1
...
1534.65 2.98 POOL L247 TENSOR_TENSOR k_BD<-k_kT,w_hmask 128x308 f32<-128x308 f32 x4 [4.79 <-ACT k_kT L311]
1535.33 0.70 DVE L397 TENSOR_SCALAR k_nmx<-k_mx 128x4 f32<-128x4 f32 x1
```

0.17 is the bare operation. The 0.43 ends at 1528.83, 0.02 us behind POOL's copy, and the 0.70 at 1536.03, 0.02 behind the second of the four pieces of BD; all 40 of the 128 scalings that took over 0.19 us end 0.02 to 0.03 us behind a POOL instruction that they had met. The Trainium skill, page "SBUF — State Buffer", section Who interferes with whom, has an exclusive lock for VectorE and GpSimd, held for a whole instruction. The 40 rows agree with it. Seven in stage 1 that began beside POOL's power (128x4) were not held and took 0.17, so not every POOL instruction does it. The rival that each scaling holds ScalarE back did not come: the doubled scaling cost less than its own time.

**Stage 1.** -4.8 against -4, a hit by luck. At the full clock a group went from 37.2 to 35.2, -2.0 where -0.6 was forecast. "Plain units: 3.66 to 3.88, +0.22, three of them" failed there: one unit went from 3.62 to 3.83, and a pair of units with a projection went from 9.2 to 8.3 in the mean, -0.9 where -0.33 was forecast. Against these 12 us stand two things that the sum did not have: two groups at a clock of 0.95 (+3) and the last group, 31.9 to 36.1 (+4.2). By the run without a bias, the bias is worth -8.7 and the rest of the change (strips, order) +3.7 (259.2 against 250.5 and 255.5). At the full clock the rest is a gain as well, 36.6 against 37.2 a group; its loss lies in four groups at 0.96 and in the last one, 33.4 in place of 31.9.

**Stage 4.** The term -36 is 29 to 32 by its reversal and 22.7 by the two profiles. VectorE's busy time in a group fell from 72.5 to 68.3 us (forecast -4.5), and the group by 31.5 / 7 = 4.5: the step "some more comes back from POOL; I take -5.2" was 0.7 too large. The rival of a POOL backlog forecast -20, and the profiles alone can't tell it from the sum; but its mechanism did not come, since TensorE's wait for the product fell from 142.2 to 115.7 us. Of the 8.8 us between 31.5 and 22.7, 7.6 lie in the trace of the kernel before (573.1 against 580.7 with the same tail). The order of the channels is excluded, and the two groups at 0.85 in that trace make up 5.7 of them.

**Openings.** -19.7, -12.8 and -4.8 against -17, -12 and -7. In stage 1 the fillers did bring the full clock to the projections, which I had counted at the low one, and then POOL's BD was late instead. In stage 4 the step of 5 us is shown by its reversal (5.1), and that it costs the first group some 2 us was left out. In stage 5 I was 2 too high.

**Fillers.** Forecast -4; 5.4 us by the medians and 9 by the ratios, on the edge of noise; by the traces 4.0, with 7 in the openings less 3 that stage 1 lost.

## What to carry to other kernels

Moving work from VectorE to ScalarE pays only until the longest loop that goes through ScalarE is the bound. Write that loop down (copy, Exp, release) beside each engine's own sum. With 128 keys the bias gained 8.7 us, and with 77 the same edit cost 17.3: it took a plain unit from 3.63 to 3.83 us with 128 and from 2.81 and 3.08 to 3.55 and 3.62 with 77, and what VectorE got back in the other units made up for that only with 128. Sum the steady groups and the last one apart: the last has no next group's work to hide a longer loop, and here it lost 4.2 and 5.4 us that the forecast did not have. Price each part by its own reversal, since two profiles can differ by some microseconds in parts that nobody edited.

## What the runs showed of the hardware that I had not expected

Where TensorE's clock falls inside a group matters more than its mean. The two stage 4 groups with the same 68.3 us on VectorE took 84.8 and 79.2 us. Both have low stretches in their second half; the first has one of 10.2 us more, 16 us behind the gate. The same part of both groups, window and then TensorE:

```profile
972.20:982.40 10.20, 8.25 (x11) 3.02 (x12) 8.71 (x16) 1.92 (x3) 5.01 (x5) 0.51 0.00 1
1057.20:1067.40 10.20, 9.28 (x23) 4.00 (x24) 9.78 (x18) 3.73 (x6) 5.25 (x6) 1.00 0.00 1
```

```profile
976.65 2.07 PE L1616 MATMUL PS<-m_hC,identf 128*128 128x512 f32 x2 [1.65 <-POOL m_hC L1362]
978.52 3.62 PE L1562 MATMUL PS<-m_xnT,m_Wc 128*128 128x512 f32 x4
...
1059.46 1.12 PE L1616 MATMUL PS<-m_hC,identf 128*128 128x512 f32 x2 [0.85 <-POOL m_hC L1362]
1060.42 1.88 PE L1562 MATMUL PS<-m_xnT,m_Wc 128*128 128x512 f32 x4
```

At 1.2 GHz the first four records of the convolution's projections (L1562) end 25.9 us behind the gate, at 2.4 GHz 21.3: that is 4.6 of the 5.6 us. With fillers, groups at a mean of 0.94 took 79.0 and 82.0, so the mean alone says little. Why the clock falls in one group and not in the other stays open: in the 16 us ahead of it TensorE was busy 13.11 and 12.80 us, at the full clock in both. In stage 1 a group takes 35.2 us at 1.00 and 36.9 at 0.95. Such groups were not in the trace of the kernel before (TensorE busy 35.3 us a group) and are in most traces of the changed one (31.8), but not in that without fillers, which has the same work; that less work brings them is likely, and not shown.

Stage 6's experts, which no edit touches, took 242.2 to 244.9 us in the eight traces of the first two sets and 268.0 to 269.7 in the four of the third, and 273.2 and 270.7 in the two first profiles. The medians of the kernel before differ by about as much (2173.4, 2173.5; 2199.8, 2202.6). So the chip, or something that goes with it, makes over 1% of the kernel's time in a stage with many loads; what it is, no run shows.
